# Second attention of a gated cross-attention kernel: two sets of score banks regrouped, TensorE's other work placed behind odd units, copies of the weighted values one unit earlier

## The reference, cut to what matters

```
# x, ctx: [32, 64, 256]; h = 8 heads of 8 rows of the 64, L = 256 columns
qh, kh, vh = layernorm(x), ctx, ctx reshaped to [B, 8, 8, 256]
qk  = einsum('bhdq,bhdl->bhql', qh, kh) / sqrt(8)        # 256 x 256 scores per head
sm  = softmax(qk, axis=-1)
ret = einsum('bhql,bhdl->bhdq', sm, vh)
x   = x + tanh(g_xattn[1]) * gamma * ret
```

## Time and profile before

| | us |
|---|---|
| median of 3 runs | 710.08 (710.06 to 710.14) |
| the profiled execution's own time | 703.4 |
| its span, first to last instruction | 701.7 |
| PE busy in the span | 621.0 (88%) |
| DVE busy in the span | 497.5 (71%) |
| ACT busy in the span | 416.4 (59%) |
| POOL busy in the span | 309.3 (44%) |

### The profile page before, as it was taken

One profiled execution on the slowest core, in us unless ns is written; L12 is line 12 of the kernel. 1 busy time (PEld: TensorE's weight loads), 2 busy tenths in 40 slices (PEclk: granted clock), 3 DMA queues, 4 the chain that ended last, 5 costly groups with the idle time before them and its releaser, 6 DMA issues. The chain is left out here.

```text
span 701.7 us, 16803 instructions
## 1 busy us (share of the span) xinstructions
PE 621.0 (88%) x5077; PEld 463.5 (66%) x5077; DVE 497.5 (71%) x885; ACT 416.4 (59%) x829; POOL 309.3 (44%) x430
## 2 busy tenths in 40 slices
PE   3788878999999858999999999999679889999995
PEld 2677757788888745555545554555367779998884
DVE  3878784788887965788888888887437744444656
ACT  3888864434344513888888888888635235555430
POOL 2456554232323367365665565553144524124254
PEclk9999988999999965999999999999959979999999
DMA  5444459100000045244434443441001325446444
GB/s 159 114 112 120 134 148 306 43 1 1 0 0 15 10 114 148 82 134 115 114 104 134 113 114 104 133 112 31 1 2 45 121 90 186 146 148 178 126 132 125
DMA packets 70370, 70.42 MB, mean 100 GB/s; under 512 B 10421, under 2 KB 66581, under 8 KB 70325
## 3 DMA queue, kind: packets, MB, share of 16 engines
q1 hardware_dynamic: 65092, 55.55, 27.2%
q0 software_dynamic: 5232, 14.29, 6.9%
HBM read 38.22 MB, written 31.33 MB: 99 GB/s over the span
## 5 line engine op out<-in xcount | busy, mean ns | idle before, releaser
L1388 DVE TENSOR_REDUCE a_smax<-a_s 128x4 f32<-128x1024 f32 x128 | 154.3, 1214 | 35.1 <-PE a_s L1315 34.6
L1200 ACT ACTIVATE a_prob<-a_st 128x512 f32<-128x512 f32 x256 | 145.1, 593 | 29.4 <-PE a_st L1310 27.3
L1310 PEld LDWEIGHTS a_st<-qop,kop 25*128 25x128 f32 x512 | 66.0, 185 | 72.2 <-issue 51.5
L1315 PE MATMUL a_s<-kop,qop 24*128 24x256 f32 x512 | 104.3, 341 | 7.1 <-DVE a_smax L1388 4.8
L1310 PE MATMUL a_st<-qop,kop 25*128 25x256 f32 x512 | 105.4, 330 | 2.4 <-ACT a_prob L1200 1.9
L1255 PE MATMUL a_pv<-a_prob,a_vt 128*32 128x256 f32 x1024 | 81.6, 391 | 5.7 <-ACT a_pv_sb L1185 5.7
L816 POOL TENSOR_TENSOR f_hs_lo<-f_kept,f_hs_hi 128x512 fp32r<-128x512 f32 x32 | 41.3, 1324 | 87.7 <-ACT f_hs_hi L766 87.7
L1315 PEld LDWEIGHTS a_s<-kop,qop 24*128 24x128 f32 x512 | 65.1, 192 | 9.5 <-DVE a_smax L1388 6.1
L1833 POOL DMA_INDIRECT sorted_rows<-m_xn,m_slot x32 | 32.9, 1029 | 49.9 <-PE m_gu L126 27.2
L124 PE MATMUL f_bank<-f_xt_hi,w_hi 128*128 128x512 f32 x128 | 51.0, 398 | 1.2 <-DVE w_raw L859 0.6
L125 PE MATMUL f_bank<-f_xt_lo,w_hi 128*128 128x512 f32 x128 | 50.3, 393 | 0.0
(11 more groups left out here) (263 smaller groups left out, 1704.1 us busy)
## 6 DMA issues: line engine op xcount, KB each, us to landing
kop<-kop_rows SPq DMA_DIRECT2D x128, 48.0 KB
qop<-qop_rows SPq DMA_DIRECT2D x128, 48.0 KB
sorted_rows<-x_all SPq DMA_DIRECT2D x2, 2944.0 KB, 15.4
expert_rows<-turned SPq DMA_DIRECT2D x46, 128.0 KB
kop_rows<-k_hi SPq DMA_DIRECT2D x32, 128.0 KB, 2.3
qop_rows<-q_hi POOLq DMA_DIRECT2D x30, 128.0 KB, 2.6
qop<-sorted_rows SPq DMA_DIRECT2D x24, 128.0 KB, 2.2
kop<-sorted_rows SPq DMA_DIRECT2D x22, 128.0 KB, 2.4
```

Source lines behind the costliest of these rows:

```text
L1200: act.activation(prob[:, u % 8], st_ps[u % 2][:], ACT.Exp, scale=SCALE1).then_inc(prob_ready, 1)
L1310: st = pe.matmul(st_ps[u % 2][:, c * D:(c + 1) * D], lhsT=kop[t.slot][strip, u // 4, c * P:(c + 1) * P], rhs=qop[t.slot][strip, u // 4], s ...
L1315: sm = pe.matmul(s_ps[j % 2][:, k, c * D:(c + 1) * D], lhsT=qop[v.slot][strip, w // 4, c * P:(c + 1) * P], rhs=kop[v.slot][strip, w // 4], ...
L1388: dve.tensor_reduce(smax[:, v.slot, opposite(2 * j):opposite(2 * j) + 2].rearrange("p u q -> p (u q)"), s_ps[j % 2][:].rearrange("p u (q n ...
```

## The change

The six score banks are now three single banks for `s_ps` and three for `st_ps`; unit u uses bank u mod 3 of each, except that unit 15 uses bank 1. Before it writes, PE waits for the exponential and for the reduction of the last unit that used that bank (`after_last_use`). DVE reduces one unit at a time, so there are 16 reductions of 512 columns per tile where there were 8 of 1024. On PE all other work stands behind odd units: `turn(t, 1)` behind 1 (was 2), `selected` behind 5 and 7 (were 6 and 8), the context transposes behind 13 (was 14). On ACT the copies of weighted values stand behind units 2, 6, 10, 14 (were 3, 7, 11, 15), that is ahead of the exponentials of 3, 7, 11, 15, and the copy to `back` behind 8 (was 9). `products` stays where it was. On DVE the statistics follow unit 3, the reciprocals units 10 and 12.

```diff
-        s_ps = [ctx.enter_context(nc.psum_tensor(f"a1_s{i}", [P, 2, 512], F32)) for i in range(2)]
-        st_ps = [ctx.enter_context(nc.psum_tensor(f"a1_st{i}", [P, 512], F32)) for i in range(2)]
+        s_ps = [ctx.enter_context(nc.psum_tensor(f"a1_s{i}", [P, 512], F32)) for i in range(3)]
+        st_ps = [ctx.enter_context(nc.psum_tensor(f"a1_st{i}", [P, 512], F32)) for i in range(3)]
...
+        BANK = [u % 3 for u in range(UNITS - 1)] + [1]
+
+        def after_last_use(eng, sem, step, u):
+
+            last = max(w for w in range(u - UNITS, u) if BANK[w] == BANK[u])
+            if last < 0:
+                after(eng, sem, step.plus(-1), UNITS, last + UNITS + 1)
+            else:
+                after(eng, sem, step, UNITS, last + 1)
@@ ScalarE's list
-                    if u == 3:
+                    if u == 2:
                         weighted(o, 3)
-                    if u == 9 and o.inside(TILES):
+                    if u == 8 and o.inside(TILES):
...
-                    if u in (7, 11, 15):
-                        weighted(t, (u - 7) // 4)
+                    if u in (6, 10, 14):
+                        weighted(t, (u - 6) // 4)
@@ TensorE's list
-                        if u >= 2:
-                            after(pe, prob_ready, t, UNITS, u - 1)
-                        else:
-                            after(pe, prob_ready, t.plus(-1), UNITS, UNITS - 1 + u)
+                        after_last_use(pe, prob_ready, t, u)
...
-                        if k == 0 and j >= 2:
-                            after(pe, smax_ready, v, PAIRS, j - 1)
-                        elif k == 0:
-                            after(pe, smax_ready, v.plus(-1), PAIRS, PAIRS - 1 + j)
+                        after_last_use(pe, smax_ready, v, u)
...
-                    if v.inside(TILES) and k == 1:
+                    if v.inside(TILES):
                         sm.then_inc(s_done, 1)
-                    if u == 2:
+                    if u in (1, 3):
+                        products(o, 3, u // 2)
+                    if u == 1:
                         def before():
                             after(pe, vt_ready, t)
                             spare()
                         turn(t, 1, before)
-                    if u in (1, 3):
-                        products(o, 3, u // 2)
                     if u % 2 and u > 3:
                         products(t, u // 4 - 1, u % 4 // 2)
-                    if u in (6, 8):
-                        selected(o, u // 2 - 3)
+                    if u in (5, 7):
+                        selected(o, (u - 5) // 2)
...
-                    if u == 14 and v.inside(TILES):
+                    if u == 13 and v.inside(TILES):
@@ VectorE's list
-                for j in range(PAIRS):
-                    if j == 4:
+                for u in range(UNITS):
+                    if u == 8:
                         negated(v, 0)
                     if v.inside(TILES):
-                        after(dve, s_done, v, PAIRS, j + 1)
-                        dve.tensor_reduce(smax[:, v.slot, opposite(2 * j):opposite(2 * j) + 2].rearrange("p u q -> p (u q)"),
-                                          s_ps[j % 2][:].rearrange("p u (q n) -> p (u q) n", q=2), AX_X, ALU.max).then_inc(smax_ready, 1)
-                    if j in (5, 6) and o.inside(TILES):
-                        cols = slice((j - 5) * P, (j - 4) * P)
+                        after(dve, s_done, v, UNITS, u + 1)
+                        dve.tensor_reduce(smax[:, v.slot, opposite(u)], s_ps[BANK[u]][:].rearrange("p (q n) -> p q n", q=2),
+                                          AX_X, ALU.max).then_inc(smax_ready, 1)
+                    if u in (10, 12) and o.inside(TILES):
+                        cols = slice((u - 10) // 2 * P, (u - 8) // 2 * P)
```

More of the change, by code:

```diff
@@ L967, in attention1 @@
     turned = keep["turned"]
-    PAIRS = UNITS // 2
     FULL = DS // P
@@ L1199, in step @@
                             act.wait_ge(shared_lo, 1)
-                        act.activation(prob[:, u % 8], st_ps[u % 2][:], ACT.Exp, scale=SCALE1).then_inc(prob_ready, 1)
+                        act.activation(prob[:, u % 8], st_ps[BANK[u]][:], ACT.Exp, scale=SCALE1).then_inc(prob_ready, 1)
                     if u == 2:
@@ L1224, in _ @@
             for dc in range(DC):
-                turned.copy(act, FIRST, dc, s_ps[0][:, dc])
+                turned.copy(act, FIRST, dc, s_ps[dc][:])
             turned.high(act, FIRST)
@@ L1287, in step @@
                 for u in range(UNITS):
-                    j, k = divmod(u, 2)
                     if t.known and t.n == 0 and u == 4:
@@ L1309, in step @@
                             strip = slice(u % 4 * UROWS, u % 4 * UROWS + KROWS)
-                            st = pe.matmul(st_ps[u % 2][:, c * D:(c + 1) * D], lhsT=kop[t.slot][strip, u // 4, c * P:(c + 1) * P],
+                            st = pe.matmul(st_ps[BANK[u]][:, c * D:(c + 1) * D], lhsT=kop[t.slot][strip, u // 4, c * P:(c + 1) * P],
                                            rhs=qop[t.slot][strip, u // 4], start=True, stop=True, tile_position=(u % 4 * UROWS, 0))
@@ L1314, in step @@
                             strip = slice(w % 4 * UROWS, w % 4 * UROWS + QROWS)
-                            sm = pe.matmul(s_ps[j % 2][:, k, c * D:(c + 1) * D], lhsT=qop[v.slot][strip, w // 4, c * P:(c + 1) * P],
+                            sm = pe.matmul(s_ps[BANK[u]][:, c * D:(c + 1) * D], lhsT=qop[v.slot][strip, w // 4, c * P:(c + 1) * P],
                                            rhs=kop[v.slot][strip, w // 4], start=True, stop=True, tile_position=(w % 4 * UROWS, 0))
@@ L1350, in _ @@
             pe.wait_ge(turned.xn_ready, 1)
-            pe.wait_ge(smax_ready, TILES * PAIRS)
+            pe.wait_ge(smax_ready, TILES * UNITS)
             for dc in range(DC):
-                turned.transpose(pe, first_xn, dc, s_ps[0][:, dc], ident)
+                turned.transpose(pe, first_xn, dc, s_ps[dc][:], ident)
         @block.vector
@@ L1370, in negated @@
                     src = smax[:, w_.slot, 8 * h:8 * h + 8].rearrange("p (g v) q -> p q v g", g=2)
-                    after(dve, smax_ready, w_, PAIRS, 4 * h + 4)
+                    after(dve, smax_ready, w_, UNITS, 8 * h + 8)
                     after(dve, neg_done, w_.plus(-1), 2, h + 1)
@@ L1394, in step @@
                         dve.reciprocal(rden[:, cols], back[:, 1, cols]).then_inc(rden_ready, 1)
-                    if j == 1 and s.known and s.n == TILES + LAG:
+                    if u == 2 and s.known and s.n == TILES + LAG:
                         turned.low(dve, FIRST)
-                    if j == 1 and p.inside(TILES):
+                    if u == 3 and p.inside(TILES):
                         after(dve, x_ready, p)
```

## The result

The changed kernel takes 747.92 us (median of 4 runs, 744.87 to 750.92) against 710.11 us before: ratio 1.053 [1.049, 1.057], 38 us slower. The sign was forecast, the size was not: 725 us, with a range up to 734.

The account below looks back on a forecast made before the run. PE was taken as the bound: 12.61 us a step with whole pairs, plus waits of 1.00, 0.48 and 0.97, less 0.1, gives 14.96 against 13.99. With the ends +15 us: 710.1 + 15 = 725 us, range 712 to 734.

Parts of the forecast that it names:

- The sign: Whole kernel: slower, at a chance of 0.81, against 0.13 for faster and 0.06 for the same.
- The bound and PE's list: Second attention: PE bounds the 13.99 us step; whole pairs save 0.96 us, leaving 12.61 us if all waits vanish.
- DVE: Reductions of 512 columns: 0.60 us each in a queue, 0.69 after waiting; DVE's step 12.6 us, or 14.1 with 0.69 throughout.
- Wait (a): At unit 1 of the next step: PE waits for unit 15's exponential, now behind a copy; 1.00 us a step.
- (b): At the products behind unit 5: PE waits for unit 3's exponential, now behind a copy; 0.48 us a step.
- (c): At unit 15: PE waits for unit 13's reduction to free the bank, behind both reciprocals; 0.97 us a step.
- The sum: Per step: 12.61 + 1.00 + 0.48 + 0.97 - 0.1 = 14.96 us against 13.99; +15 us in all.
- the clock: Rival: more and longer PE gaps drop the granted clock to 1.2 GHz in the stage; 28 us more, 753; chance 0.03.
- a third of the stage: Term of the clock rival: the share of the stage assumed at the low clock, 0.33 in its 28 us.
- 1.4 times the step: Term of the clock rival: the step's assumed length at the low clock, entering its 28 us as 0.4.

Follow-up runs that it names:

- e4: Changed kernel with ACT's copies back at their old units and the reciprocals behind units 11 and 13: 704.49 us, 0.991 of the kernel before.
- e2: Changed kernel with ACT's copies back at their old units (3, 7, 11, 15, back at 9): 707.84 us, 0.992 of the kernel before.
- e6: Kernel before with only ACT's copies moved up a unit (2, 6, 10, 14, back at 8): 855.73 us, 1.214 of the kernel before.
- e14: Kernel before with ACT's copies moved up a unit, plus 5 spare matmuls behind unit 0 and 4 behind unit 4: 769.81 us, no ratio given.
- e1: Changed kernel with 13 more spare matmuls a step, behind units 0, 5 and 13: 721.15 us, 1.015 of the kernel before.
- e11: Changed kernel without the six spare matmuls of a step: 773.57 us, 1.086 of the kernel before.
- e15: Changed kernel, copies at old units, reciprocals behind 11 and 13, old spares out, 4 spare matmuls behind unit 0: 701.44 us, 0.986 of the kernel before.
- e7: Kernel before without the six spare matmuls of a step: 692.61 us, 0.982 of the kernel before.
- e16: Kernel before without the six spare matmuls of a step, run again in a later series: 698.93 us, 0.982 of the kernel before.

## Why the prediction was wrong

- *The bound and PE's list.* Right as far as the runs go: undoing the added waits (e4) gave a faster kernel. Mis-sized: a pair costs 0.62 us only behind products; behind transposes or `selected` it takes 0.45 (343.65 to 344.10). I had seen it in one row and took 0.1 us for it in all; three such pairs a step save 0.5.
- *DVE.* 0.60 in a queue, 0.68 on average over 224. Right. By the Trainium skill (VectorE: DVE Perf Modes, the section on the TRN2 errata) I had estimated 0.66 for a single one; the measured 0.68 to 0.69 alone is nearer to that than the 0.60 in a queue.
- *Wait (a)* 1.00 forecast, 0.95 measured; *(b)* 0.48 and 0.62; *(c)* 0.97 and 1.05. Mechanism and place right, sizes close; each was undone by an experiment of its own or with its neighbour.
- *The sum.* 14.96 us a step forecast, 14.46 measured at full clock. Two errors partly cancel, which is luck. In the step shown PE's list is some 0.8 us shorter than I put it: by the pairs, and by 0.1 each time `selected` follows products (0.45, 345.91 to 346.36, not 0.57). The waits are 0.4 longer, 0.2 of it at the products behind unit 9 (349.06), which wait for the exponential of unit 7 and which I had counted as nothing. Order and banks alone would by this have given some 717 us.
- *The step that failed: the clock.* "Against it: from 503 to 507 us PE is busy 1.09 of 4 us and the clock is still 1.00, while the new gaps are about 1 us." What stands behind that row refutes the use I made of it:

```profile
503.08 1.09 PE L273 MATMUL a_s<-ident,a_vt 128*128 128x128 f32 x8 [0.55 <-DVE a_vt L173]
512.89 2.27 PE L1563 MATMUL m_gu<-m_wr,turned 128*128 128x8 f32 x10 [8.72 <-DMA m_wr<-in_L_ffn_W_router]
```
```profile
507.00:511.00 4.00, 0.00 (x0) 0.00 (x0) 0.85 (x2) 0.00 (x0) 0.02 (x1) 0.60 0.00 0
```

PE did nothing from 504.17 to 512.89, and the clock fell in that time, 0.8 us behind the end of my row ((1.00 - 0.60)/0.50 x 4 = 3.2 of its 4 us are at the low level). The row ended before the fall, so it was no evidence that the clock survives quiet times; nor did it hold what the change makes, short waits between busy stretches. I had priced this rival at 28 us on top of the three waits (753), with a chance of 0.03 and outside the range, and left it out of the sum. It came true: 83 of 231 us at the low level, 28.7 us. That the two sizes agree is partly luck, for "a third of the stage" and "1.4 times the step" were not worked out from rows. The section of the Trainium skill that I named (TensorE: Matmul & The Clock Gate, "A second HAM failure mode: psum-queue depth-cycling") tells of small gaps while banks are cycled, and of a clock that goes to and fro; the trace agrees (PE busy 1.68 to 2.36 of 3 us ahead of falls, nine stretches at 0.50). The cycling of banks alone does not do it: e2 and e4 cycle through the same three at 1.00.

Open: why the clock of e6 stays low, from 362 us to beyond the end of the steps, where that of the changed kernel returns within 4 to 14 us. The busy share of the profile does not tell: e14 shows PE busy 40.00 of 40 us at 0.50 (300 to 340).

## What to carry to other kernels

Before an in-order engine's instruction is moved ahead of another, ask what it waits for and whether the instruction now behind it feeds what it waits for: a copy moved up one unit here put an exponential behind a product, and cost about 1 us a step on TensorE. Where TensorE's list is close to the bound, price each new wait twice, at its length and at what the clock does behind it, above all where two of them lie side by side; and look at the clock in the rows behind a quiet stretch too. Spare matmuls that hold the clock belong in or beside the place where the engine stands (e1, e11, e15); in a kernel without such a place they were only work (e7).

## What was not expected of the hardware

- Five copies moved by one unit took the granted clock from 1.00 to 0.50 for the rest of the stage (e6: 24.4 us a step instead of 14). Between the two lies no edit of any matmul.
- More matmuls made the kernel faster (e1: 13 more a step, 748 to 721 us).
- Score matmuls of a pair of units take 0.44 to 0.49 us behind transposes or `selected`, and 0.57 to 0.62 behind products, though `selected` and products have the same shape.
- A kernel can be 11 us faster in ten runs and 86 us slower in the eleventh (e7 and e16: 690.15 to 707.07, and 796.85).
